# Cross-attention on one core: scores with the keys stationary, VectorE block transposes for the probabilities, and a value product on half the PE rows

## What is computed

```python
q = (query @ Wq + bq).reshape(B, L, NKV, G, HDIM)
k_, v_ = jnp.split(kv @ Wkv + bkv, 2, axis=-1)
scores = jnp.einsum('blkgd,bmkd->bkglm', q, k) * scale
attn = jax.nn.softmax(scores, axis=-1)
o = jnp.einsum('bkglm,bmkd->blkgd', attn, v).reshape(B, L, NHEAD * HDIM)
x = x + (o @ Wo + bo)
h = jnp.einsum('nd,erd->ner', flat, A)
hw = h * w[:, :, None]                  # w: gates of the top 2 of 8 experts
out = jnp.einsum('ner,eor->no', hw, Bm) * SCALING
```

## Time and profile before

| | |
|---|---|
| time, median of three executions | 1196.17 us (1193.82 to 1199.01) |
| span of the profiled execution | 1190.4 us |
| PE busy | 98% of the span, 6093 matmuls |
| DVE, ACT, POOL busy | 54%, 37%, 33% |
| granted clock of TensorE, mean | 0.990 |
| start, to the first scores | 219.25 us |
| 30 units between the scores of the second and of the last | 246.10 to 1100.46 us, 28.48 us each |
| tail, from the scores of the last unit | 90 us |

### The profile page before, as it was taken

One profiled execution on the slowest core, in us unless ns is written; L12 is line 12 of the kernel. 1 busy time (PEld: TensorE's weight loads), 2 busy tenths in 40 slices (PEclk: granted clock), 3 DMA queues, 4 the chain that ended last, 5 costly groups with the idle time before them and its releaser, 6 DMA issues.

```text
span 1190.4 us, 16458 instructions
## 1 busy us (share of the span) xinstructions
PE 1160.9 (98%) x6093; PEld 987.3 (83%) x6093; DVE 641.0 (54%) x1084; ACT 438.6 (37%) x730; POOL 397.7 (33%) x323
## 2 busy tenths in 40 slices
PE   7999999799999999999999999999999999999987
PEld 5888888688888888888888888888888888888785
DVE  4454552355555555555555555555555555556966
ACT  3111211443443344334434344444344344433320
POOL 2331451423443244224423342424244324422200
PEclk9999999899999999999999999999999999999988
DMA  8545545220212120202110121112021212121003
GB/s 292 177 124 190 165 124 132 63 80 28 62 27 63 28 62 26 62 26 68 36 54 26 62 62 26 27 61 62 26 71 34 62 26 62 27 46 27 1 2 142
DMA packets 56182, 81.58 MB, mean 69 GB/s; under 512 B 8608, under 2 KB 25032, under 8 KB 56144
## 3 DMA queue, kind: packets, MB, share of 16 engines
q1 hardware_dynamic: 56144, 81.06, 22.9%
HBM read 60.07 MB, written 20.97 MB: 68 GB/s over the span
## 4 chain that ended last, share of the span: by engine, by line
PE 93%; DVE 3%; DMA 2%; ACT 1%; issue 0%; SPq 0%; POOL 0%; DVEq 0%
PE ring L908 25%; PE ring L910 24%; PE ring L909 24%; PE att L1000 5%; PE att L999 5%; PE att L1022 3%; PE att L1023 2%; PE turn L1010 2%; PE turn L921 2%; DMA v_raw<-values_dram 1%; DMA raw<-in_L_xattn_Wkv_dram 1%; DVE pT L631 1%; DVE y L716 1%; PE att L909 0%; PE att L910 0%
## 5 line engine op out<-in xcount | busy, mean ns | idle before, releaser
L908 PE MATMUL ring<-xT_h,w_h 128*128 128x512 f32 x512 | 202.8, 396 | 0.0
L908 PE MATMUL ring<-wo_h,oT_h 128*128 128x512 f32 x512 | 202.2, 395 | 0.0
L910 PE MATMUL ring<-xT_h,w_l 128*128 128x512 f32 x512 | 200.0, 391 | 0.0
L910 PE MATMUL ring<-wo_h,oT_l 128*128 128x512 f32 x512 | 200.0, 391 | 0.0
L909 PE MATMUL ring<-xT_l,w_h 128*128 128x512 f32 x512 | 199.9, 390 | 0.0
L909 PE MATMUL ring<-wo_l,oT_h 128*128 128x512 f32 x512 | 199.4, 389 | 0.0
L720 DVE SCALAR_TENSOR_TENSOR qT_l<-ring,g_bias,qT_h 128x512 fp32r<-128x512 f32 x128 | 96.0, 750 | 171.9 <-ACT qT_h L502 170.9
L716 DVE TENSOR_TENSOR y<-ring,y 128x512 f32<-128x512 f32 x144 | 99.2, 691 | 139.7 <-PE ring L910 139.6
L502 ACT ACTIVATE qT_h<-ring,g_bias 128x512 fp32r<-128x512 f32 x128 | 88.2, 689 | 164.5 <-PE ring L910 164.1
L501 ACT ACTIVATE pT<-turn 64x512 fp32r<-64x512 f32 x128 | 76.0, 594 | 145.5 <-PE turn L1010 143.9
L437 POOL TENSOR_TENSOR s_mem<-s_mem,row_max 128x512 f32<-128x512 f32 x64 | 67.3, 1051 | 180.3 <-DVE row_max L705 180.3
(11 more groups left out here) (118 smaller groups left out, 1986.3 us busy)
## 6 DMA issues: line engine op xcount, KB each, us to landing
v_raw<-values_dram SPq DMA_DIRECT2D x64, 256.0 KB, 3.9
raw<-in_L_xattn_Wkv_dram SPq DMA_DIRECT2D x8, 1024.0 KB, 6.3
values_dram<-s_mem SPq DMA_DIRECT2D x64, 128.0 KB, 2.5
keys_dram<-s_mem SPq DMA_DIRECT2D x32, 256.0 KB, 2.5
raw<-in_L_xattn_Wq_dram SPq DMA_DIRECT2D x8, 1024.0 KB, 5.9
k_raw<-keys_dram SPq DMA_DIRECT2D x32, 256.0 KB, 3.1
raw<-in_L_xattn_Wo_dram SPq DMA_DIRECT2D x8, 1024.0 KB, 5.2
y<-in_ctx_dram SPq DMA_DIRECT2D x16, 256.0 KB, 4.5
```

The costliest lines, as they stand in the source:

```text
L908: mm(dst, stat[0], mov[0], start=start, stop=False)
L910: return mm(dst, stat[1], mov[0], start=False, stop=stop)
```

## The change

- **Scores.** The keys of a batch, high and low beside each other, are now the stationary side (128 columns: 64 high, 64 low), and all 4 heads of the batch the moving side, 256 columns: 2 matmuls for each batch in place of 4. The result has keys on the partitions (high in 0 to 63, low in 64 to 127) and the queries along the free dimension. An even batch takes the first half of a bank, an odd one the second.
- **Adding high and low.** ACT copies the half that is wanted elsewhere, for even and odd batches apart (`copy_half`, 2 instructions on 64 partitions for each chunk), and DVE adds (`s_add`, 2 instructions on 64 partitions), so that the even batch of a pair lies in partitions 0 to 63 of `sT` and the odd one in 64 to 127.
- **Softmax.** DVE turns `sT` in blocks of 32x32 (`nc.vector.transpose`), which puts 32 of the 64 keys of a query in a row. The maximum and the sum over 64 keys are then joined from two partial ones in neighbouring quarters of the partitions: ACT exchanges them (`swap`, 4 copies of 32x16 numbers, for the maximum and for the sum, in each chunk), DVE joins them (`s_peak`, `s_inverse`). After `normalise` DVE turns back (`p_turn`).
- **Probabilities.** No transposes on PE any more, and none of their 4 splits on 64 partitions on ACT and DVE. ACT writes the high part (`probs_high`, one instruction of 128x512 a chunk), POOL the low part (`probs_low`).
- **Value product.** An even and an odd batch lie in the two halves of the partitions: each matmul uses 64 rows, and the halves write different banks. Three passes (high by high, low by high, high by low), 12 matmuls of 256 columns in each of two chunks. Chunk 0 stands after the third query head, chunk 1 after the fourth; both write `turn`.
- **Orders.** `v_high` and its low part go to the end of the unit on ACT and POOL, the split of the next Wq on POOL ahead of the softmax. `v_raw` is loaded once, in pieces of 128 numbers. DVE's order in the softmax is longer, and add_out(3) stands between `p_turn(0)` and `p_turn(1)`. The special order of the second unit is gone.

```diff
             def shift(u, c):
-                pool.wait_ge(max_done, u * 2 + c + 1)
+                pool.wait_ge(peak_done, u * 2 + c + 1)
...
+            def probs_low(u, c):
+                pool.wait_ge(p_high, u * 2 - 1 + c)
+                low(chunk_of(pT_l, c), sT[:, c * D:(c + 1) * D], chunk_of(pT_h, c)).then_inc(p_low, 1)
...
+                if not first:
+                    probs_low(u, 0)
+                    probs_low(u, 1)
                 if T == 1:
                     split_wo(step)
                 pool.wait_ge(k_high, u + 1)
-                low(kT[:, 1], k_raw[:], kT[:, 0]).then_inc(k_low, 1)
-                pool.wait_ge(v_high, u + 1)
-                low(v_l[:], v_raw[:], v_h[:]).then_inc(v_low, 1)
+                low(kT[:, :, 1, :], k_raw[:], kT[:, :, 0, :]).then_inc(k_low, 1)
+                if T == UNITS - 1 and not last_group:
+                    for c in range(KC):
+                        split_w(step + 1, c)
...
                 shift(u, 1)
...
                 normalise(u, 1)
...
+                pool.wait_ge(v_high, u + 1)
+                low(v_l[:], v_raw[:], v_h[:]).then_inc(v_low, 1)
...
+            def swap(dst, src, blocks):
+                for q in (0, 2):
+                    act.copy(dst[q * QR:(q + 1) * QR, blocks], src[(q + 1) * QR:(q + 2) * QR, blocks])
+                    last = act.copy(dst[(q + 1) * QR:(q + 2) * QR, blocks], src[q * QR:(q + 1) * QR, blocks])
+                return last
+            def copy_half(u, c):
+                act.wait_ge(scores_filled, u * 4 + 2 * c + 2)
+                banks = slice(2 * c, 2 * c + 2)
+                act.copy(half[L:P, c], att_s[L:P, banks, 0, :])
+                act.copy(half[0:L, c], att_s[0:L, banks, 1, :]).then_inc(half_copied, 1)
...
+                copy_half(u, 0)
+                copy_half(u, 1)
+                swap_max(u, 0)
+                swap_max(u, 1)
+                exponents(u, 0)
+                exponents(u, 1)
+                swap_sum(u, 0)
+                swap_sum(u, 1)
                 act.wait_ge(v_loaded, u * 32 + 32)
                 high(v_h[:], v_raw[:]).then_inc(v_high, 1)
...
+            def s_add(u, c):
...
+                whole = sT[:, cols].rearrange("p (n q) -> p n q", n=2)
+                nc.vector.tensor_tensor(whole[0:L], att_s[0:L, banks, 0, :], half[L:P, c], ALU.add)
+                nc.vector.tensor_tensor(whole[L:P], att_s[L:P, banks, 1, :], half[0:L, c], ALU.add).then_inc(s_added, 1)
...
+                nc.vector.transpose(low_or_x[:, cols], sT[:, cols]).then_inc(s_turned, 1)
+                dve.wait_ge(s_turned, u * 2 + c + 1)
                 nc.vector.tensor_reduce(row_max[:, blocks], s[:, blocks, :], AX, ALU.max).then_inc(max_done, 1)
...
+                s_add(u, 0)
                 s_max(u, 0)
+                s_add(u, 1)
+                s_peak(u, 0)
                 s_max(u, 1)
+                add_out(1)
+                s_peak(u, 1)
+                s_sum(u, 0)
+                add_out(2)
+                s_inverse(u, 0)
+                s_sum(u, 1)
+                s_inverse(u, 1)
+                p_turn(u, 0)
...
                 add_out(3)
+                p_turn(u, 1)
...
                 for b in range(UB):
-                    for hp in range(HP):
-                        dst = att_s[:, b * HP + hp]
-                        q_h, q_l = (q[:, b, 2 * hp:2 * hp + 2, :].rearrange("p h l -> p (h l)") for q in (qT_h, qT_l))
-                        mm(dst, q_h, kT[:, :, b, :], start=True, stop=False)
-                        last = mm(dst, q_l, kT[:, :, b, :], start=False, stop=True)
+                    dst = att_s[:, b // 2, b % 2, :]
+                    q_h, q_l = (q[:, b].rearrange("p h l -> p (h l)") for q in (qT_h, qT_l))
+                    mm(dst, kT[:, b].rearrange("p i l -> p (i l)"), q_h, start=True, stop=False)
+                    last = mm(dst, kT[:, b].rearrange("p i l -> p (i l)"), q_l, start=False, stop=True)
...
+            def outputs(u, c, banks):
                 pe.wait_ge(v_low, u)
+                pe.wait_ge(p_low, u * 2 - 1 + c)
+                for n in range(2 * c, 2 * c + 2):
+                    for v, p in ((v_h, pT_h), (v_l, pT_h), (v_h, pT_l)):
+                        for i in range(2):
+                            keys_of = slice(i * L, (i + 1) * L)
+                            last = mm(banks[:, i, n % 2 * G * L:(n % 2 + 1) * G * L], v[keys_of, n, :], p[keys_of, n, :],
+                                      start=p is pT_h and v is v_h, stop=p is pT_l)
...
+                for h in range(G - 1):
+                    queries(g, T, u, h)
                 if not first:
...
+                    outputs(u, 0, turn)
+                queries(g, T, u, G - 1)
...
+                    outputs(u, 1, turn)
                     out_project(u, out_task(u, 0), out_slot(0), 0)
                 scores(u, first)
```

More of the change, by code:

```diff
@@ L38 @@
 UB = UTOK // L
+PAIRS = UB // 2
+QR = 32
 UT = UTOK // P
@@ L466, in unit @@
                 shift(u, 1)
-                if T == UNITS - 1 and not last_group:
-                    split_w(step + 1, 0)
                 normalise(u, 0)
                 normalise(u, 1)
-                if T == UNITS - 1 and not last_group:
-                    for c in range(1, KC):
-                        split_w(step + 1, c)
+                pool.wait_ge(v_high, u + 1)
+                low(v_l[:], v_raw[:], v_h[:]).then_inc(v_low, 1)
             for j in range(STEPS):
@@ L492, in _ @@
                 unit(NKV - 1, T, False)
+            probs_low(NU, 0)
+            probs_low(NU, 1)
             root("f", TILES - 8)
@@ L541, in unit @@
                 last_group = isinstance(g, int) and g == NKV - 1
-                second = isinstance(u, int) and u == 1
-                if not first and not second:
-                    probs_high(u)
+                if not first:
+                    probs_high(u, 0)
                 if T == 0:
@@ L604, in _ @@
                 if kind == "PV":
-                    probs_high(NU)
+                    probs_high(NU, 0)
+                    probs_high(NU, 1)
                 elif kind == "O":
-                    outputs_high(NU)
+                    for c in range(2):
+                        outputs_high(NU, c, att[:, 2 * c:2 * c + 2])
                 elif kind == "f":
@@ L750, in unit @@
                     dve.wait_ge(bias_ready, g + 1)
-                second = isinstance(u, int) and u == 1
-                if not first and not second:
-                    probs_low(u)
-                query_low(u, 0)
-                if second:
-                    dve.wait_ge(resid_ready, TILES)
-                    probs_low(u)
-                    query_low(u, 1)
-                if not first:
-                    outputs_low(u)
-                if not second:
-                    query_low(u, 1)
-                for h in range(2, G):
-                    query_low(u, h)
+                for h in range(G - 1):
+                    query_low(u, h)
+                if not first:
+                    outputs_low(u, 0, turn)
+                query_low(u, G - 1)
+                if not first:
+                    outputs_low(u, 1, turn)
+                if isinstance(u, int) and u == 1:
+                    dve.wait_ge(resid_ready, TILES)
                 if isinstance(g, int) and g == NKV - 1 and T >= 2:
@@ L889, in _ @@
                     low(bm_l, ring[:, n % 2, :], bm_h).then_inc(ring_emptied, 1)
-                elif kind == "PV":
-                    probs_low(NU)
                 elif kind == "O":
-                    outputs_low(NU)
+                    for c in range(2):
+                        outputs_low(NU, c, att[:, 2 * c:2 * c + 2])
                 elif kind == "R":
@@ L1001, in scores @@
+                    q_h, q_l = (q[:, b].rearrange("p h l -> p (h l)") for q in (qT_h, qT_l))
+                    mm(dst, kT[:, b].rearrange("p i l -> p (i l)"), q_h, start=True, stop=False)
+                    last = mm(dst, kT[:, b].rearrange("p i l -> p (i l)"), q_l, start=False, stop=True)
                     if b % 2:
                         last.then_inc(scores_filled, 1)
-            def turn_probs(u, first):
-                for c in range(2):
-                    pe.wait_ge(probs_ready, u * 2 + c + 1)
-                    if not first:
-                        pe.wait_ge(p_low, u * 2)
-                    for b in range(4 * c, 4 * c + 4):
-                        last = nc.tensor.transpose(turn[:, c, (b % 4) * P:(b % 4 + 1) * P],
-                                                   s[:, HP * b:HP * b + HP, :].rearrange("p k l -> p (k l)"), ident[:])
-                    last.then_inc(p_turned, 1)
@@ L1027, in unit @@
             def unit(g, T, first):
                 u = g * UNITS + T
-                second = isinstance(u, int) and u == 1
-                queries(g, T, u, 0)
-                if second:
-                    turn_probs(0, True)
-                    queries(g, T, u, 1)
```

(14 more changed lines are left out.)

199 lines of the change are left out of this document (104 added, 95 removed).

## The result

The changed kernel takes 1213.2 us (1212.68 to 1214.89, four executions), the kernel before 1195.7 us in the same job: a ratio of 1.0148, with a 95% interval of 1.013 to 1.0166. Forecast were 1163 us and a range of 1135 to 1212. The sign was wrong, and the time lies just outside the range.

What follows compares the result with a forecast made beforehand. PE's matmuls bound the kernel, 28.48 us a unit; afterwards PE work plus waits give 27.4. So 1190.4 - 1 + 30 x (27.4 - 28.48) = 1157, with 5.8 outside the span 1163 us; 8-in-10 range 1135 to 1212.

Steps and rivals of the forecast that it cites:

- What bounds the kernel before: In mid-kernel no wait ends on PE; a unit of 28.48 us costs what its matmuls cost.
- What PE saves: PE's work per unit: scores and transposes get cheaper, the sum becomes 25.6 us, 2.9 less, if nothing waits.
- V: Value product's PE time per unit, halves side by side, changes of kind included: 1.85 us, ends 1.44 and 3.3.
- changes of kind: On PE around the value product: four more switches between kinds of matmul per unit, 0.1 each, 0.4 us in all.
- Where the chain is tied to PE: PE waits for ring banks at out_project 3 (1.4 us idle) and the next unit's second query head (14.3 to 14.5).
- The size of the chain: Softmax chain over ACT, DVE and POOL from a unit's scores to add_out(3): 14.5 us, making a unit 27.3, then 27.4.
- overlaps: On the chain, some instructions overlap by 0.08 where nothing is awaited, so add_out(3) was taken at 14.5, not 14.7.
- The break-even: With V at 1.85, add_out(3) at 15.5 us after the scores' start would make a unit as long as before.
- rival (2): Slower through the chain to add_out(3): transposes at 1.2 add 1.5 us, exchanges at 0.83 add 0.8; both 1232; chance 0.21.
- Hidden things: Rest of the loop costs nothing, v_raw in small pieces included; only Wo at T = 1 adds 0.1 to 0.2 a unit.
- The ends: First unit gains 4 us (scores at 214.5, then about 27.5 to the second), tail loses 3: together -1.
- the 5.8 us: Work outside the profiled span that the change does not touch: the executions' median is 5.8 us over the span.

Runs made afterwards that it cites:

- values_early: next_head_early with Wo's high-part split shared with ACT, all low parts on POOL, and the values' split moved ahead of POOL's normalisation: 1139.26 us, ratio 0.9541.
- next_head_early: The changed kernel with all three adds to y and the next unit's first query head taken out earlier, g_bias copied at a group's end: 1165.94 us, ratio 0.9764.

## Why the prediction was wrong, step by step

- **What bounds the kernel before**: right. Its units are 28.45 to 28.55 without idle time on PE, so all of the change's worth had to come from PE's work.
- **What PE saves**: nearly right. Scores 16 in 1.92 us (505.26 to 507.18). The sum was 25.6 forecast; values_early shows 26.03, 2.45 less than before. The mis-sized term is V: 2.2 in place of 1.85. The pairs cost the 0.12 forecast; the changes of kind were put at 0.4 in all, from the transposes' 0.32, and cost nearly 0.8: in each chunk 0.09 ahead of the first pair, 0.10 on the first, 0.09 on the last and 0.11 on the matmul after it.
- **Where the chain is tied to PE**: right in kind. Both places are the ones named. Add_out(1) ran from 8.3 to 9.0 (forecast its end at 8.8), PE idle for 1.51 (1.4).
- **The size of the chain: the step that failed.** The exchange was priced at 0.55, from large instructions that overlap by 0.07, against 0.83 from the lone small instruction of the earlier trace rows. It is 0.84. Three of them stand in the path: 0.87 of the 1.1 us by which add_out(3) was late (its end at 15.6, forecast 14.5). The other 0.2 is what the prediction took off its own list, which ended at 14.7, for overlaps: 14.7 and 0.87 are the 15.6 that came. The break-even that the prediction itself gave was 15.5. With V and the start-up of PE after each idle time, 13.34 from the second head to the next scores in place of 12.8, a unit is 29.0 and not 27.4. Of the 1.7 us the exchanges are 0.9, the overlaps 0.2, V 0.35, and the rest is in PE's matmuls: the first behind the stop takes 0.33 in place of 0.23, others a few ns more than 0.228. With the exchanges alone at 0.84 the prediction's own sum gives 28.2, still a little under the kernel before. The upper bound was in the text, but rival (2) gave "exchanges at 0.83" as +0.8 and left that case beside the forecast, where it was the likeliest: the only row of about the same size was that lone one. What came is rival (2) in a mild form, to which the prediction gave 0.21. The other reading was at hand too: the splits on 64 partitions in the earlier trace rows, four in 2.42, take 0.58 each in the trace of before and start 0.61 apart, so they don't overlap either.
- **Idle time costs more than the bracket says.** From start to start the two stops hold 1.51 and 0.83 of idle time, 0.16 each by which PE's rows otherwise overlap, and 0.11 each for the slower first matmul: 2.9, and 26.03 + 2.9 is 28.9 of the 29.0.
- **Hidden things**: right. `v_raw` in small pieces, kT, the splits at T = 3 cost nothing; Wo at T = 1 cost 0.2.
- **The ends**: the first scores came at 214.2 (forecast 214.5), a gain that is hard to tell apart from the scatter of the start; the first unit then took 29.6 and not 27.5. The tail lost 5.1 and not 3: in the last unit add_out(3) also stands behind a layer-norm tile and three sets of statistics, and PE waited 4.12 us for it before the small transposes at 1135.06. Together +2.8 in place of -1. This did not show in the sum, by luck: the 5.8 us that the prediction added for work outside of the span were mostly scatter between executions (in each execution of before and after that has a span beside its time, the two are 1.7 to 2.1 apart), and that error was as large, the other way. The miss of 50 us is 30 units times 1.68.
- **Where the expected gain went**: of 2.45 us of PE work saved in a unit, 2.9 were given back as waits for ring banks. It was not lost in the operations that the change added: the same operations, in another order, gave 1139 us.

## What to carry to other kernels

When work moves from the busiest engine to a chain over three others, look at what else stands in those engines' lists: an in-order list ties every buffer it empties to the chain. Empty the buffers of the busiest engine ahead of the step that waits, all of them up to the next one it needs, since moving only some moves the idle time on and may join two short ones into one that costs the clock. Price a new small instruction by a row of its own size, not by the overlap of large ones.

## What was unexpected of the hardware

Small ACT copies (32x16) start 0.21 apart and take 0.20, and the copies of 64x512 start 0.59 apart and take 0.58, where one does not wait for the other; activations of 128x512 that wait for nothing overlap by about 0.10 (`oT_h`, 0.60 long, start 0.50 apart). So it is not the number of columns: those that did not overlap are on 32 or 64 partitions, those that did on all 128. Why is open. The Trainium skill (ScalarE: Activation LUTs, What ACT_TABLE_LOAD costs) says that ACTIVATEs back to back overlap by about 93 ns; the rows agree for those on 128 partitions and not for these copies.

Some DVE instructions that have all their operands in SBUF were stretched beside POOL. The copy of `g_bias` (128x4) took 0.60 us in after, where POOL's `v_l` ran, and ended each of the seven times some 0.03 us after it; it took 0.16 in next_head_early, where POOL was idle. ACT waited 8.9 us in all for seven of them, for their place in DVE's list as well as for their length. In the tail of after a `tensor_scalar` on 128x4 took 1.14 beside POOL's `pT_l`; before it was 0.17 in all eight places:

```profile
1136.39 0.16 DVE L715 TENSOR_TENSOR rstd<-stats 128x4 f32<-128x4 f32 x1
1136.58 1.14 DVE L717 TENSOR_SCALAR mean<-mean 128x4 f32<-128x4 f32 x1
...
1136.36 1.32 POOL L424 TENSOR_TENSOR pT_l<-s_mem,pT_h 128x512 fp32r<-128x512 f32 x1 [1.39 <-ACT pT_h L510]
```

The two `wo_l` of DVE above, 1.66 each, look like the same thing; with PSUM as a source the same subtraction takes 0.69. The Trainium skill (SBUF — State Buffer, SBUF: two separate sides) says that DVE operations in a two-port mode, or with two SBUF inputs against a GpSimd operation that reads SBUF, share one pair of ports with GpSimd, and that whichever starts first holds it for its whole instruction. The traces agree for the copies and the tensor_scalar, which end when POOL's instruction does. They don't for the first row, a sum of two SBUF inputs that by the profile, which is rough for POOL, started 0.03 us after POOL's instruction and was not stretched. The block transposes (0.71) and the reductions (0.69), with one SBUF input, were not stretched beside POOL either.
